# Keeping the second norm's mean out of the stored rows, spreading the side work, and starting the seven products with the raw quarters

## What is computed

```python
# L0_attn_x: [16, 2048, 2048]
def attn(x, W, b):                      # W: [4096, 2048]
    gates, values = jnp.split(jnp.einsum('btc,dc->btd', x, W) + b, 2, axis=-1)
    # hidden[t] = sigmoid(gates[t]) * hidden[t-1] + tanh(values[t])
    return associative_scan(_scan_op, (sigmoid(gates), tanh(values)), axis=1)[1]

def ffn(x, w_fc, w_proj):               # w_fc: [5120, 2048], w_proj: [2048, 5120]
    h = jnp.einsum('bsd,hd->bsh', x, ternarize_weight(w_fc))    # -a, 0 or a; a = mean |w|
    h = jnp.square(jax.nn.relu(h))
    return jnp.einsum('bsh,dh->bsd', h, ternarize_weight(w_proj))

x = x + _layernorm(attn(_layernorm(x), W, b))
x = x + _layernorm(ffn(_layernorm(x), w_fc, w_proj))
```

## Time and profile before

| | |
|---|---|
| median of 3 runs (lowest to highest) | 3450.22 us (3200.65 to 3568.2) |
| the profiled execution: its own time | 3199.74 us |
| its slowest core (core 1), span | 3198.2 us |
| the other cores' spans | 3154.8 to 3186.3 us |
| PE busy in that span | 2999.9 us, 94% |
| DVE, ACT, POOL busy | 1718.0 us (54%), 1410.1 us (44%), 308.8 us (10%) |
| DMA | 564.59 MB, 177 GB/s on average |
| first stage | start to about 1123 us |
| quarter 0 | about 1123 to 1289 us |
| quarters 1 to 7 | about 1289 to 2214 us |
| last stage | from there to 3198 us |

### The profile page before, as it was taken

How to read it: one execution, slowest core, us unless ns; L and a number is a source line. 1 busy time by engine, 2 the same in 40 slices (tenths; PEclk the granted TensorE clock), 3 DMA queues, 4 the chain that set the end, 5 groups by cost and what they waited for, 6 DMA issues and landing times.

```text
span 3198.2 us, 53789 instructions; the slowest of 8 cores (3154.8 to 3198.2 us)
## 1 busy us (share of the span) xinstructions
PE 2999.9 (94%) x20660; PEld 2046.7 (64%) x20660; DVE 1718.0 (54%) x2440; ACT 1410.1 (44%) x2150; POOL 308.8 (10%) x454
## 2 busy tenths in 40 slices
PE   3889999998999979999899999999999999999997
PEld 2778888887788834768577686785444444444443
DVE  2355555666676528523567667652454454454454
ACT  2446665554555447677556666663111111111111
POOL 0011111111111111111011111110000000000000
PEclk8999999999999989999999999999999999999999
DMA  7968887778777798364555746627433333333231
GB/s 224 303 191 253 274 275 238 216 235 234 212 230 216 217 186 271 119 198 137 151 158 154 183 128 187 161 74 255 173 120 116 106 119 114 103 119 121 95 125 69
DMA packets 303807, 564.59 MB, mean 177 GB/s; under 512 B 150080, under 2 KB 196288, under 8 KB 289472
## 3 DMA queue, kind: packets, MB, share of 16 engines
q1 hardware_dynamic: 267680, 401.74, 43.8%
q0 software_dynamic: 35872, 159.40, 14.1%
HBM read 372.85 MB, written 154.66 MB: 165 GB/s over the span
## 4 chain that ended last, share of the span: by engine, by line
PE 71%; DMA 7%; DVE 7%; SPq 5%; issue 5%; ACT 4%; POOL 1%; DVEq 0%; ACTq 0%; POOLq 0%
PE psA L112 44%; PE psB L112 27%; SPq L108 5%; DMA slab<-wfc 4%; DVE st L100 3%; DMA slab<-wpj 1%; PE psB L144 1%; DVE xr L120 1%; POOL s L136 1%; DVE q L136 1%; DMA slab<-W 1%; ACT slab L92 1%; ACT qst L92 1%; ACT gt L92 1%; DVE hTr L140 1%
## 5 line engine op out<-in xcount | busy, mean ns | idle before, releaser
L112 PE MATMUL psA<-xnT,wt 128*128 128x256 bf16 x8192 | 940.3, 278 | 66.8 <-DMA xnT<-xn 34.4
L112 PEld LDWEIGHTS psA<-xnT,wt 128*128 128x128 bf16 x8192 | 813.8, 100 | 178.2 <-issue 72.3
L112 PE MATMUL psA<-xn1T,wq 128*128 128x512 bf16 (+1 forms) x2512 | 433.4, 332 | 30.5 <-ACT zb L92 23.2
L112 PEld LDWEIGHTS psA<-xn1T,wq 128*128 128x128 fp8e4 x2512 | 246.9, 98 | 204.5 <-issue 35.6
L112 PE MATMUL psA<-w,hs 128*128 128x512 fp8e4 x1600 | 349.9, 379 | 0.0
L112 PE MATMUL psB<-w,hs 128*128 128x512 fp8e4 x1600 | 349.9, 379 | 0.0
L140 DVE TENSOR_TENSOR_SCAN hTr<-gt,hTr 128x256 f32<-128x256 f32 x248 | 184.1, 743 | 283.8 <-ACT hTr L92 283.8
L112 PE MATMUL psB<-xn1T,wq 128*128 128x256 bf16 (+1 forms) x1824 | 283.0, 313 | 8.8 <-DVE xn1T L136 8.8
L112 PEld LDWEIGHTS psB<-w,hs 128*128 128x128 bf16 x1600 | 156.6, 98 | 188.8
L112 PEld LDWEIGHTS psA<-w,hs 128*128 128x128 bf16 x1600 | 156.5, 98 | 188.8
L112 PEld LDWEIGHTS psB<-xn1T,wq 128*128 128x128 fp8e4 x1824 | 180.0, 99 | 101.2 <-issue 12.7
(11 more groups left out here) (76 smaller groups left out, 3442.9 us busy)
## 6 DMA issues: line engine op xcount, KB each, us to landing
slab<-wfc SPq DMA_DIRECT2D x160, 512.0 KB, 6.8
slab<-wpj SPq DMA_DIRECT2D x160, 512.0 KB, 4.7
pc<-h_s SPq DMA_DIRECT2D x64, 640.0 KB, 5.1
h_s<-hst_b POOLq DMA_DIRECT2D x140, 256.0 KB, 3.1
xr<-x POOLq DMA_DIRECT2D x32, 1024.0 KB, 9.2
x_s<-xr POOLq DMA_DIRECT2D x32, 1024.0 KB, 7.8
xb<-x_s SPq DMA_DIRECT2D x64, 512.0 KB, 4.4
xin<-x SPq DMA_DIRECT2D x31, 1024.0 KB, 6.0
```

The source lines that it names most:

```text
L112: return lambda e: e.matmul(*a, **k)
```

## The change

1. The mean term of the second norm (nm2) is kept for all 32 row tiles as a column of one tile. Part b of `Back` is gone: no ACT pass over the row, x1_s is stored by t_, and the table loses its b entries; q moves up a slot (4 and 11). At the output `ln4` adds the column to bs4, one DVE instruction of 128 x 1.
2. Steps of ROWS move from slots 0, 1, 2, 3, 8, 9, 10, 11 to 0, 2, 3, 4, 8, 10, 11, 12, so the normed row is two slots behind its statistics; t_ of tt = 0 stays one slot behind.
3. `scan` puts the recurrence on DVE right away, ahead of the rest of the preparation in its slot. The tern pass takes slots 1, 5, 6, 9, 12, 13, 14, 15, and slots 5 and 9 take a second slab, behind the recurrence.
4. `mean_abs` waits for the last abs instruction (acc_end), not for all that ACT has been given, and has two more yields ahead of its product.
5. x3_load(1) comes as one DMA transpose each at ht = 15, 21, 27 and 33.
6. `seven` takes its products in the order 5, 2, 3, 1, 7, 4, 6, not 3, 1, 5, 7, 4, 2, 6, with as many copies (4) and additions (8).
7. The rates of `prep_two` change a little, and the last two plain products of a quarter get none.

```diff
@@ -386,7 +387,7 @@
                 while len(ahead) < min(3, len(srcs) - n):
                     ahead.append(slab_load(srcs[n + len(ahead)]))
                 i, t = ahead.pop(0)
-                slab_free[i] = ACT.do(op.activation(out=stage[i], in_=stage[i], func=AF.Abs,
+                acc_end[0] = slab_free[i] = ACT.do(op.activation(out=stage[i], in_=stage[i], func=AF.Abs,
                                                     accum_out=acc[:, n:n + 1]), t, acc_free[0])
                 yield
 
@@ -438,10 +439,12 @@
         def mean_abs(n, am, thr, nthr):
 
             t = DVE.do(op.tensor_reduce(out=amc["red"][:, :], in_=acc[:, 0:n], axis=AX.X, op=ALU.add),
-                       (ACT.sem, ACT.n))
+                       acc_end[0])
             acc_free[0] = t
             ones = stage[0][:, 0:P]
             t = DVE.do(op.memset(ones, 1.0), slab_free[0])
+            yield
+            yield
             yield
             key, bank = next_bank()
             slab_free[0] = t = PE.do(op.matmul(bank[:, 0:1], ones, amc["red"][:, :], start=True, stop=True),
@@ -598,9 +601,6 @@
             t = ACT.do(op.activation(out=hT(k, j, 0, CHA), in_=bank[:, CHA:2 * CHA], func=AF.Tanh,
                                      bias=bT[:, NP + j:NP + j + 1]), hT_free[i])
             bank_free[key] = t
-            return lambda: scan_do(k, j, n, init, t, t0)
-
-        def scan_do(k, j, n, init, t, t0):
             t = DVE.do(op.tensor_tensor_scan(
                 out=hT(k, j, 0, CHA), data0=gt[n][:, :], data1=hT(k, j, 0, CHA), initial=init,
                 op0=ALU.mult, op1=ALU.add), t, t0)
...
@@ -645,22 +646,16 @@
 
             def t_(self, tt):
                 buf = self.buf[tt]
+                row = self.k * TA + tt
                 self.tn = DVE.do(op.scalar_tensor_tensor(
-                    out=s1["nm2"][:, :], in0=sm["mv2"][:, 0:1], scalar=-1.0, in1=s1["rs2"][:, :],
-                    op0=ALU.mult, op1=ALU.mult), self.t[tt], free["nm2"])
+                    out=nm2[:, row:row + 1], in0=sm["mv2"][:, 0:1], scalar=-1.0, in1=s1["rs2"][:, :],
+                    op0=ALU.mult, op1=ALU.mult), self.t[tt])
                 t = DVE.do(op.scalar_tensor_tensor(
                     out=buf[:, :], in0=psB[:, :], scalar=s1["rs2"][:, :], in1=buf[:, :],
                     op0=ALU.mult, op1=ALU.add), self.t_x[tt])
                 for b in range(4):
                     bank_free["B", b] = t
                 free["rs2"] = self.t[tt] = t
-
-            def b(self, tt):
-                row, buf = self.k * TA + tt, self.buf[tt]
-                t = ACT.do(op.activation(out=buf[:, :], in_=buf[:, :], func=AF.Identity,
-                                         bias=s1["nm2"][:, :]), self.t[tt])
-                free["nm2"] = self.t[tt] = t
-                DVE.wait(self.tn)
                 x1_mark[row] = POOL.dma(d_st[buf is xr2], op.dma_start(out=x1_d[row], in_=buf[:, :]), t)
 
             def s3(self, tt):
@@ -802,9 +797,11 @@
                 zm[r, c] = ACT.do(op.copy(out=zb[z][:, :], in_=bank), t, z_free[z])
                 return zm[r, c]
 
-            def add(r, c, bank, t, o=ALU.add):
-                z = zb[zi[r, c]]
-                zm[r, c] = DVE.do(op.tensor_tensor(out=z[:, :], in0=z[:, :], in1=bank, op=o), t, zm[r, c])
+            def add(r, c, bank, t, how="add"):
+
+                z = zb[zi[r, c]][:, :]
+                a, b, o = {"add": (z, bank, ALU.add), "sub": (z, bank, ALU.subtract), "rsub": (bank, z, ALU.subtract)}[how]
+                zm[r, c] = DVE.do(op.tensor_tensor(out=z, in0=a, in1=b, op=o), t, zm[r, c])
                 return zm[r, c]
 
             def finish(r, c):
...
@@ -830,28 +827,28 @@
                             t = PE.do(f)
                         else:
                             PE.quiet(f)
+                if m == 5:
+                    put(1, 2, bank, t)
+                    bank_free[key] = put(1, 1, bank, t)
+                if m == 2:
+                    put(2, 1, bank, t)
+                    bank_free[key] = put(2, 2, bank, t)
                 if m == 3:
-                    put(1, 2, bank, t)
-                    bank_free[key] = put(2, 2, bank, t)
+                    add(1, 2, bank, t)
+                    bank_free[key] = add(2, 2, bank, t, "rsub")
+                    finish(1, 2)
                 if m == 1:
-                    DVE.wait(put(1, 1, bank, t))
+                    add(1, 1, bank, t, "rsub")
                     bank_free[key] = add(2, 2, bank, t)
-                if m == 5:
-                    add(1, 2, bank, t)
-                    bank_free[key] = add(1, 1, bank, t, ALU.subtract)
-                    finish(1, 2)
                 if m == 7:
                     bank_free[key] = add(1, 1, bank, t)
                 if m == 4:
-                    DVE.wait(put(2, 1, bank, t))
-                    bank_free[key] = add(1, 1, bank, t)
+                    add(1, 1, bank, t)
+                    bank_free[key] = add(2, 1, bank, t)
                     finish(1, 1)
-                if m == 2:
-                    add(2, 1, bank, t)
-                    bank_free[key] = add(2, 2, bank, t, ALU.subtract)
                     finish(2, 1)
                 if m == 6:
-                    bank_free[key] = add(2, 2, bank, t, ALU.subtract)
+                    bank_free[key] = add(2, 2, bank, t, "sub")
                     finish(2, 2)
                 yield
             st_end[0] = t
@@ -988,6 +985,7 @@
             mb = DVE.do(op.scalar_tensor_tensor(
                 out=s1["bs4"][:, :], in0=sm["mv4"][:, 0:1], scalar=-1.0, in1=s1["sc4"][:, :],
                 op0=ALU.mult, op1=ALU.mult), m, free["bs4"])
+            mb = DVE.do(op.tensor_tensor(out=s1["bs4"][:, :], in0=s1["bs4"][:, :], in1=nm2[:, t:t + 1], op=ALU.add), mb)
             w = 1024 // pieces
             for i in range(2):
                 x = xb[i]
@@ -1070,11 +1068,11 @@
         step(ROWS)
 
 
-        BACK = {0: "x0", 2: "s0", 3: "t0", 4: "b0", 5: "q0", 6: "n0", 7: "x1 s1", 10: "t1", 11: "b1", 12: "q1", 13: "n1"}
+        BACK = {0: "x0", 2: "s0", 3: "t0", 4: "q0", 6: "n0", 7: "x1 s1", 10: "t1", 11: "q1", 13: "n1"}
 
         def back_do(back, parts):
             for p in parts.split():
-                part = {"x": back.x, "s": back.s, "t": back.t_, "b": back.b, "q": back.s3, "n": back.n3}[p[0]]
+                part = {"x": back.x, "s": back.s, "t": back.t_, "q": back.s3, "n": back.n3}[p[0]]
                 part(int(p[1]))
 
         def back_slot(back, j):
...
@@ -1121,10 +1119,8 @@
             for j in range(NP):
                 if k == 2 and j == 0:
                     first, back = back, Back(1)
-                    back_do(first, "q1")
+                    back_do(first, "n1")
                     trans(1, 0, range(13))
-                if k == 2 and j == 1:
-                    back_do(first, "n1")
                 back_slot(back, j)
                 if j >= 13:
                     trans(k, 0, range(11) if j == 13 else [j - 3])
@@ -1132,24 +1128,22 @@
                     if j == 4:
                         xn1T_free[0] = wt_read[1]
                         x3_load(0)
-                elif j in (0, 1, 2, 3, 8, 9, 10, 11):
+                elif j in (0, 2, 3, 4, 8, 10, 11, 12):
                     step(ROWS)
-                twice = phase[0] == "tern" and j in (13, 15)
+                twice = phase[0] == "tern" and j in (5, 9)
                 if phase[0] != "tern":
                     step(PREP, (k, j) > (2, 0))
-                elif j in (1, 4, 6, 9, 11, 13, 14, 15):
+                elif j in (1, 5, 6, 9, 12, 13, 14, 15):
                     step(PREP)
                 if last and j in (11, 13):
                     wq_load((j - 11) // 2)
                 g = gemm1(k, j)
                 back_late(back, j)
-                do = scan(k, j, *g)
-                for _ in range(1 + twice):
-                    if half[0]:
-                        step(PREP)
-                    if _ < twice:
-                        step(PREP)
-                do()
+                scan(k, j, *g)
+                if half[0]:
+                    step(PREP)
+                if twice:
+                    step(PREP, 2)
             back = Back(k)
         drain(PREP)
         xn1T_free[1] = wt_read[NP - 1]
@@ -1166,8 +1160,8 @@
                 back_slot(back, ht)
                 if ht == NP - 1:
                     a_end = (PE.sem, PE.n), (DVE.sem, DVE.n), (ACT.sem, ACT.n), *q_free
-            if ht == 6:
-                x3_load(1)
+            if ht in (15, 21, 27, 33):
+                x3_load(1, [(ht - 15) // 6])
             if ht % 4 == 1 and ht < 32:
                 wq_load(2 + ht // 4)
             if 17 <= ht < 17 + NS:
@@ -1196,7 +1190,7 @@
             for g in range(0, NS, 2):
                 for n, _ in enumerate(seven(q, g)):
                     if not last and n < 6:
-                        prep_two(0.33 if phase[0] == "abs" else 0.27)
```

(4 more changed lines are left out.)

21 lines of the change are left out of this document (11 added, 10 removed).

## The result

The changed kernel is faster, by 1.3%: ratio to the kernel before 0.9874, 95% interval 0.9838 to 0.9911. The forecast was 3097 us with a range of 3062 to 3145 us. The profiled execution took 3165.74 us, the median is 3161.69 us. The time lies outside the range, on the slow side, and 1.3% is within the 2% that the prediction called about no change. In some executions the cores of one die, or of both, have a lower granted clock and take longer (3447.55 us for this kernel); the ratios leave these out, and for e6, whose profiled execution has one such die, the cores of the other are read.

The account below looks back on a forecast made before the run. PE, busy 94% of the span, was taken as the bound, with about 198 us of gaps where it waits for other engines. From 3199.74 us, 54 + 5 + 5 + 20 + 19 - 0.2 = 103 us gives 3097 us, range 3062 to 3145.

Parts of the forecast that it names:

- First stage, 54 us: Slot 13 of chunk 2 to slot 13 of chunk 15: 72 us lost, 54 regained; ends 25 and 72.
- Rival 3: First stage: other loads make ACT and DVE as late; only waits outside go, 49 us; 3151 us; chance 0.09.
- the loss left: First stage: late slab loads still cost PE 1.4 us per chunk with the clock's share, 18 us of the 72.
- Chunk 2, 5 us: Chunk 2, PE's 3.85 us wait for psB: slab loads start earlier; gain 5 us with the clock, 0 to 7.
- Behind the first stage, 44 us: After the first stage: 20 us from quarter 0's transposes, 19 from the order of seven products, 5 from mean_abs.
- the transposes of quarter 0: Quarter 0: single DMA transposes in place of four together remove PE's 21.84 us gap; gain 20 us, ends 10 and 24.
- the seven's order: Starts of quarters 4 to 6: the new order covers PE's waits for t_make; gain 19 us, ends 10 and 22.
- The mean product's wait: End of quarter 2: PE's 10.60 us wait shortens; gain 5 us, some 6 us of wait remain.
- Rival 2: Quarter 0: transposes bound by the engines, not the queue, giving about 10 us, not 20; 3107 us; chance 0.12.
- Rival 4: Groups of seven products: new order makes ACT late; slower, 3269 us at 3.5 us per group; chance 0.03.
- Rival 1: First stage: slab loads become the limit, 29 us more lost in tern chunks; 3126 us, or 3136; chance 0.15.

Follow-up runs that it names:

- e6: Changed kernel with the rows' norm back in slots 1 and 9, load and transpose left in slots 3, 4, 11, 12: ratio 0.9770 to the kernel before.
- e5: Changed kernel with the rows' norm issued ahead of the second norm's step in slots 2 and 10, slots unchanged: ratio 0.9799 to the kernel before.
- e12: Changed kernel with the norm left in slots 2 and 10, the load behind it in the same slots, the transpose in 3 and 11: ratio 0.9971.
- e9: Kernel before with only the rows' steps moved to slots 0, 2, 3, 4, 8, 10, 11, 12: ratio 1.0234, 75 us slower.
- e1: Changed kernel with the rows' steps back in slots 0 to 3 and 8 to 11: 3102.22 us, ratio 0.9655 to the kernel before.
- e4: Changed kernel with both the rows' steps and the tern pass's slab slots as before: ratio 0.9746 to the kernel before.
- e7: Changed kernel with quarter 0's four transposes issued together at head tile 6, as before: ratio 0.9930 to the kernel before.
- e8: Changed kernel with the old order of the seven products and the old rates of slab work: ratio 0.9945 to the kernel before.
- e10: Changed kernel with only the old order of the seven products, new rates of slab work kept: ratio 0.9969 to the kernel before.
- e11: Changed kernel with the rows' steps in their old slots and no slab in slot 11 of the abs pass: 3094.83 us, ratio 0.9640.

## Why the prediction was wrong

**First stage, 54 us: wrong, and this is most of the miss.** The measured gain in the 13 chunks is -0.7 us (some 55 us short), behind them it is 10 us short. The steps that failed, as the prediction put them:

- "Moved within the chunk: DVE's columns and statistics, about 3 us, into slots with nothing else." Slot 10 did not hold nothing: it holds the 2.34 us scaling, and the norm's column stands behind it. I had looked at the rows' steps as work of DVE, and not at ACT, whose norm waits in order ahead of that slot's gate and tanh. e5 prices the column's place: 32 us of the 62.
- "It holds the queue 5.6 us, so some 8 us stay for its landing: nothing to pay." I asked when the moved transpose lands, and not what is queued behind it and behind the load of xin, which itself waits for the norm. e12 shows SP idle for 8.4 us and slab loads behind; e6 shows 95 us fewer slab waits in the tern pass when the norm alone is back, and 45 us less time. The other half of the sentence, that product 0 finds its tokens, held but for one wait of 3.74 us on core 6; on the kernel before (e9) it did not.
- "A transpose stands two slots behind its own product, 7.2 us, less 1.7 us for ACT's two instructions and the recurrence, so lateness up to 5.5 us costs PE nothing." This takes ACT and DVE to run right behind PE. In the chunk shown they run three slots behind at slot 13: the products of slot 12 are done and the gate of slot 10 is read at 924.50. DVE has worked without a gap from 908.78 to 922.3, so it has no slack to make lateness good. (Rival 3 counts 7 us of slack per transpose, where the same paragraph's working gives 5.5.)

The other edits of the first stage gave what was asked of them. Without the move the 13 chunks took 789.6 us in e1, 62 us fewer than before, with 54 forecast; e1 and e4 show the spacing of slabs at 31 us of it. That the loss left is 18 us, as forecast (789.6 less 772), is luck: the prediction had it in slots 12 to 1 of the tern pass, where e1 has 2 us, and e1 loses the other 15 in the abs pass.

**Chunk 2, 5 us**: slot 13 of chunk 2 is reached 2.7 us earlier on the mean, within its 0 to 7; e7, e8 and e10, with the same code up to there, reach it 0.3 to 1.6 us earlier, so the gain is hardly clear of the scatter.

**Behind the first stage, 44 us** (20 + 19 + 5): 34 us on the mean of the cores, 43 on the two slowest ones (2087 to 2044). By parts: the transposes of quarter 0 at 8 to 18 us (forecast 20, ends 10 and 24), the seven's order at 18 to 30 (forecast 19, ends 10 and 22), but by order alone and not by rates. The 20 us were sized by the worst core: its 21.84 us stand against 11.9 on the mean of the eight. The mean product's wait is 5.1 us shorter, with 5 forecast. The parts undone one by one sum to more than the 34 us (12 + 24 + 5 = 41); e8's 18 in place of e10's 24 would close that. The single transposes held the queue for 3.7 to 8.7 us each on the eight cores, within the 9.7 I allowed.

**The rivals.** Rival 2 (the edit gives 10 us and not 20, because the engines are full) is not settled: the 8 to 18 us measured take in its 10. In the window 1160 to 1200 us, where the share was 1.12 and the core moved 208 GB/s, the changed kernel has

```profile
1160.00:1200.00 40.00, 40.00 (x187) 18.13 (x185) 17.44 (x19) 28.32 (x46) 6.28 (x9) 1.00 1.01 325
```

PE is never idle there, at 325 GB/s and a share of 1.01. But this window has one transpose and the start of a second, the other had all four, so the two shares do not decide it alone. In favour of the queue stands that in the kernel before the first slab load behind the four transposes went out at 1181.11 and its abs instruction began at 1186.40:

```profile
1181.11 1.46 SPq L108 DMA_DIRECT2D slab<-wpj  x3
```

That is 5 us for the load, and most of the rest of the 28.84 us went by while the transposes held the queue. Why these hold the queue so long, no run here shows. The Trainium skill (Trainium Kernel Development and Optimization, Key Constraints) states that transfers issued from SP, ACT and POOL all run on the same 16 DMA engines, and that issuing from several engines at once saves only issue time. This edit leaves the four transposes on SP and only spreads them, so e7 speaks neither for that sentence nor against it. Rival 4 has only a trace of a sign: PE waits inside the groups of seven for copies and additions, 0 to 2.6 us in all on a core, where the kernel before has none on five of its cores and 1.4 to 1.7 us on three. Rival 3 comes closest: only the waits outside the first stage went, 3151 us, with 3165.74 measured (its 49 us take in the 5 of chunk 2). Its mechanism, though, was not that other loads take the place of the old ones, but that one of the edits makes them late. Rival 1 is a part of it by its sign (ACT waits over 5 us for slabs) but in the tern pass not by its cause: e1 and e6 have the same loads at a higher rate, with chunks of 59.4 us. For the abs pass it stays open.

The sum of the forecast would have been near for the kernel without the move: 3097 us forecast, 3102.22 and 3094.83 us measured in e1 and e11. Its parts were off both ways, 62 us where 54 were forecast and 29 where 44 were. The fault was to put the chance of an unpriced edit, one line among several, inside a rival of 0.09.

## What to carry to other kernels

When a step is moved by one slot, follow it through each in-order list that it stands in: what stands behind it on the engine that does it, and what stands behind the transfers that it lets go. In these traces a load that waited for a buffer held every load behind it on its queue, so the instruction that frees the buffer is on the path of transfers that have nothing to do with it. And slack counted from the program's order (two slots behind) is real only if the trace shows the other engines that close: read on the timeline how far they lag at that place.

## What the hardware showed that I had not expected

A short gap of PE can cost more than its length. After the wait of 2.61 us the next 32 matmuls took 5.95 us in place of 3.66. The granted clock (the column before the last two) is 0.50 there, the lower of its two levels (1.2 and 2.4 GHz), and 1.00 from 932.46 on:

```profile
926.56:930.50 3.94, 3.94 (x20) 2.81 (x19) 3.73 (x8) 1.59 (x3) 0.90 (x1) 0.50 0.92 204
```

After a wait of 4.72 us in e1 (core 0) it was

```profile
262.35 0.45 PE L144 MATMUL psB<-id_sb,hTr 128*128 128x128 f32 x1 [4.72 <-DVE hTr L140]
262.78 6.28 PE L112 MATMUL psA<-xnT,wt 128*128 128x256 bf16 x32
...
269.01 3.66 PE L112 MATMUL psA<-xnT,wt 128*128 128x256 bf16 x32
```

6.28 us, and the following 32 again 3.66. It isn't so behind every gap: after 1.25 us (e5, core 5, at 252.09) and after 3.30 us (e1, core 0, at 935.29) the next 32 matmuls took 3.65 us. Over the 13 chunks PE's longer busy time is 25 us of the 67. And four transposes of the same kind held a queue for 38.86 us before, 26.22 in e7 and 13.37 at the end of quarter 2: what such an instruction costs a queue is not fixed. That it depends on what else is in flight is my guess; no run here varied that by itself.
